# The first norm and split moved into edge counting, and counting in steps of six chunks, in a four-layer graph network on one core

## What is computed

```
h = relu(layernorm(x))
agg = segment_sum(h[src], dst);  cnt = segment_sum(1, dst)
y = agg / max(cnt, 1) @ W_l.T + b_l + h @ W_r.T
x = x + relu(batchnorm(y)) + h
```

## Time and profile before

| | us |
|---|---|
| median of 3 runs (1279.17 to 1279.27) | 1279.27 |
| the profiled execution, its own time | 1277.57 |
| its span, first to last instruction | 1275.8 |
| TensorE busy | 1146.9 (90%) |
| VectorE busy | 930.5 (73%) |
| ScalarE busy | 715.2 (56%) |
| GpSimd busy | 65.1 (5%) |
| first counting matmul starts | 28.08 |
| last tile of counts closed | 161.87 |
| first aggregation matmul starts | 193.63 |

### The profile page before, as it was taken

How to read it: one execution, slowest core, us unless ns; L and a number is a source line. 1 busy time by engine, 2 the same in 40 slices (tenths; PEclk the granted TensorE clock), 3 DMA queues, 4 the chain that set the end, 5 groups by cost and what they waited for, 6 DMA issues and landing times. The chain is left out here.

```text
span 1275.8 us, 17226 instructions
## 1 busy us (share of the span) xinstructions
PE 1146.9 (90%) x6001; PEld 721.6 (57%) x6001; DVE 930.5 (73%) x1686; ACT 715.2 (56%) x902; POOL 65.1 (5%) x115
## 2 busy tenths in 40 slices
PE   3999959997898995979999999969979999999996
PEld 2666634554775553434444544436536777777775
DVE  5999955002755787788989897875337888888885
ACT  1132267303556675337788786845126777777774
POOL 3000042100001200000000000000000000000000
PEclk8999968998999997989999999989989999999999
DMA  4000000003003000203111100000020011110002
GB/s 152 5 1 1 1 1 1 1 1 120 13 1 92 2 1 0 83 23 141 45 43 43 44 22 1 3 1 1 1 50 13 15 26 26 27 26 14 14 1 81
DMA packets 24770, 36.17 MB, mean 28 GB/s; under 512 B 11874, under 2 KB 13204, under 8 KB 24694
## 3 DMA queue, kind: packets, MB, share of 16 engines
q1 hardware_dynamic: 24694, 35.14, 9.1%
HBM read 26.03 MB, written 2.70 MB: 23 GB/s over the span
## 5 line engine op out<-in xcount | busy, mean ns | idle before, releaser
L59 PE MATMUL wide<-arena 125*125 (+9 forms) x2124 | 470.8, 371 | 34.0 <-DVE arena L904 13.3
L59 PEld LDWEIGHTS wide<-arena 125*125 (+5 forms) x2124 | 262.1, 131 | 219.3 <-issue 114.2
L1736 PE MATMUL wide<-arena 125*65 125x512 f32 (+1 forms) x480 | 182.3, 516 | 0.0
L1352 PE MATMUL wide<-ident,arena 125*125 125x125 f32 (+3 forms) x954 | 129.6, 282 | 14.0 <-ACT arena L603 4.7
L734 ACT ACTIVATE arena<-arena,b 125x1250 f32<-125x1250 f32 x80 | 106.7, 1336 | 60.1 <-PE wide L1736 56.0
L1251 DVE TENSOR_TENSOR arena<-wide,arena 125x1250 f32<-125x1250 f32 x80 | 116.7, 1459 | 30.1 <-PE wide L1726 30.0
L1352 PEld LDWEIGHTS wide<-ident,arena 125*125 125x125 f32 (+3 forms) x954 | 114.3, 185 | 24.5 <-issue 10.5
L813 ACT ACTIVATE arena<-wide 125x1000 f16<-125x1000 f32 x80 | 80.8, 1010 | 80.8 <-PE wide L1352 80.8
L1736 PEld LDWEIGHTS wide<-arena 125*65 125x65 f32 x480 | 63.4, 138 | 101.7 <-issue 95.3
L1313 DVE SCALAR_TENSOR_TENSOR arena<-wide,arena 125x1000 f16<-125x1000 f32 x80 | 95.9, 1198 | 33.9 <-ACT arena L813 33.9
L828 ACT ACTIVATE arena<-arena,neg_max,unit 125x1250 f32<-125x1250 f32 x80 | 114.3, 1429 | 10.7 <-DVE neg_max L1340 10.7
(11 more groups left out here) (250 smaller groups left out, 1236.5 us busy)
## 6 DMA issues: line engine op xcount, KB each, us to landing
arena<-rows_kept SPq DMA_DIRECT2D x16, 625.0 KB, 5.9
arena<-arena SPq DMA_DIRECT2D x40, 156.2 KB, 2.9
arena<-in_L_gnn_W SPq DMA_DIRECT2D x3, 1024.0 KB, 7.7
x_nm<-in_x SPq DMA_DIRECT2D x2, 1250.0 KB
out<-x_nm SPq DMA_DIRECT2D x1, 2187.5 KB
arena<-in_L_gnn_W_l SPq DMA_DIRECT2D x1, 1024.0 KB, 5.4
arena<-in_L_gnn_W_r SPq DMA_DIRECT2D x1, 1024.0 KB, 7.9
arena<-in_L_gnn_Wk SPq DMA_DIRECT2D x1, 1024.0 KB, 5.3
```

The source lines that it names most:

```text
L59: mm = pe.matmul(ps[0:rows, lo:hi], lhsT, rhs[:, lo:hi], start=start, stop=stop, skip_group_check=True)
L1352: return pe.transpose(dst, src, ident[0:k, 0:k])
L1736: m = pe.matmul(psW[1][0:VA, lo:hi], v_gat[0:ROWS, t, h, :], ring[n % RINGS][0:ROWS, lo:hi], start=(t == 0), stop=(t == TILES - 1))
```

## The change

- The bounds: each chunk's largest and smallest target, four chunks in each of 40 partitions, are compared with the tiles' edges there; TensorE turns the 0/1 result to one row per tile (10 partitions), where first and last chunk and the number of steps are found. Two small matmuls turn these to one partition and make the running sum.
- Counting: steps of six chunks, from each tile's own first chunk; columns behind the last chunk hold -1. The ring has six places. Counts of the preceding tile are turned after the first step (two parts) and after closing (the third). The last tile's mask is made by VectorE after counting.
- TensorE turns the weights after the bounds' small matmuls.
- Norm: statistics of two x tiles in each of tiles 1 to 5, their end in tiles 6 and 7; ScalarE takes the root in tile 5 and makes h and its upper part in tiles 6 to 8 (three, three, four tiles). h has ten places. VectorE makes seven lower parts right after its last chunk, three after the split of the degrees.
- The barrier between counting and aggregation is gone; the flag for counts over 2048 has a semaphore of its own, waited for at the end of the first block. GpSimd widens tiles 1 and 6 (also in the second layer), from when all turned counts are read, and adds h to x three tiles at a time behind that. h is transposed after each tile of the second aggregation block.

The diff, cut to its core:

```diff
-CHUNKS = 4
-GROUPS = E // (CHUNKS * CHUNK)
+CHUNKS = E // CHUNK
+PER = 4
+PARTS = CHUNKS // PER
+BODY = 6
+STEPS = (CHUNKS + BODY - 1) // BODY
+PADDED = CHUNKS + 2 * BODY
...
-        BY_ACT = (0, 1, 2, 3, 4, 6, 7, 8)
-        BY_POOL = (5, 9)
+        BY_ACT = (0, 2, 3, 4, 5, 7, 8, 9)
+        BY_POOL = (1, 6)
...
@@ block.gpsimd @@
+            pool.iota(order[0:TILES, 0, :].rearrange("p (g c) -> p g c", g=PER), pattern=[[1, PER], [PER, PARTS]], base=1, **many)
+            pool.iota(order[0:TILES, 1, :].rearrange("p (g c) -> p g c", g=PER), pattern=[[-1, PER], [-PER, PARTS]], base=CHUNKS, **many)
+            pool.iota(steps_at[0:TILES, :], pattern=[[BODY, STEPS - 1]], base=BODY, **many)
+            done(pool.memset(below[:, :], float(BODY)))
+            done(pool.affine_select(out=below[:, :], in_=below[:, :], compare_op=ALU.is_ge, fill=0.0, base=-1,
+                                    pattern=[[1, TILES + 1]], channel_multiplier=-1))
...
-            phase_end(pool, 1)
-            for t in range(TILES):
-                pool.wait_ge(S["h_made"], t + 1)
-                pool.tensor_tensor(x_nm[0:ROWS, t, :], x_nm[0:ROWS, t, :], h32[0][t % len(h32[0])][0:ROWS, :], ALU.add).then_inc(S["x_plus_h"], 1)
-            widen(0)
+            pool.wait_ge(S["counts_turn_read"], 3 * TILES)
+            for k in range(KD):
+                widen(0, k)
+                for t in range(3 * k, min(3 * k + 3, TILES)):
+                    pool.wait_ge(S["h_made"], t + 1)
+                    pool.tensor_tensor(x_nm[0:ROWS, t, :], x_nm[0:ROWS, t, :], h32[0][t][0:ROWS, :], ALU.add).then_inc(S["x_plus_h"], 1)
...
@@ block.scalar @@
+            for t in range(TILES):
+                act.wait_ge(S["tile_counted"], t + 1)
...
+                copy(cnt_f[t % 3][0:ROWS, :], psW[t % 2][0:ROWS, 0:N], accum_out=deg_col[0:ROWS, t:t + 1]).then_inc(S["counts_f32"], 1)
+                if t >= 1:
+                    turned_counts(t - 1, 2)
+                if t < TILES - 1:
+                    act.activation(mask[0:ROWS, t, :], psW[t % 2][0:ROWS, 0:N], ACT.Relu, bias=bar_c[0:ROWS, :], scale=-BARRED).then_inc(S["mask_made"], 1)
+                for r in range(2):
+                    turned_counts(t, r)
+                if t == 5:
+                    take_root(ROWS, 0, TILES)
+                if t == 6:
+                    act.wait_ge(S["ln_ready"], 1)
+                if 6 <= t <= 8:
+                    norm_first(*(range(0, 3), range(3, 6), range(6, TILES))[t - 6])
+            turned_counts(TILES - 1, 2)
...
@@ block.vector: bounds @@
+            tt(within[0][0:PARTS, :, :], chunk_most[0:PARTS, :].unsqueeze(2).to_broadcast(shape), edges[0], ALU.is_ge)
...
+            dve.wait_ge(S["edge_turns"], 1)
+            dve.wait_ge(S["consts_set"], 3)
+            done(tt(ordered[0:TILES, :, :], psS[1][0:TILES, 0:CHUNKS].unsqueeze(1).to_broadcast([TILES, 2, CHUNKS]), order[0:TILES, :, :], ALU.mult))
+            done(dve.tensor_reduce(ends2[0:TILES, :], ordered[0:TILES, :, :], AX, ALU.max))
+            first_c, n_steps, width, last_c = (span2[0:TILES, i:i + 1] for i in range(4))
+            ts(first_c, ends2[0:TILES, 1:2], -1.0, float(CHUNKS), ALU.mult, ALU.add)
+            done(ts(last_c, ends2[0:TILES, 0:1], 1.0, -1.0, ALU.max, ALU.add))
+            done(tt(first_c, first_c, last_c, ALU.min))
+            done(tt(width, last_c, first_c, ALU.subtract))
+            done(ts(passed[0:TILES, :], steps_at[0:TILES, :], width, None, ALU.is_le))
+            done(dve.tensor_reduce(n_steps, passed[0:TILES, :], AX, ALU.add))
+            ts(n_steps, n_steps, 1.0, 2.0, ALU.add, ALU.max).then_inc(S["edge_steps"], 1)
...
@@ block.vector: counting @@
+            for t in range(TILES):
+                if 1 <= t <= HEAD_HALF:
+                    x_stats(2 * t - 2)
+                    s = x_stats(2 * t - 1)
...
+                with dve.Fori(start, end, BODY) as n:
+                    for g in range(BODY):
+                        dve.wait_ge(S[f"hot{g}_free"], n + BODY)
+                        ts(hot_src[0:ROWS, g, :], iota_h[0:ROWS, :], e_col[0:ROWS, 1, c + g, :], None, ALU.is_equal)
+                        ts(hot_dst[0:ROWS, g, 0:ROWS], iota_h[0:ROWS, t * ROWS:(t + 1) * ROWS],
+                           e_col[0:ROWS, 0, c + g, :], None, ALU.is_equal).then_inc(S[f"hot{g}_made"], BODY)
...
@@ block.vector: after counting @@
+            for t in range(TILES - 3):
+                lower_part(0, t)
             dve.wait_ge(S["counts_f32"], TILES)
             split_cols(dve, done, parts[0:ROWS, :, :], split_rest[0:ROWS, :], deg_col[0:ROWS, :]).then_inc(S["deg_split"], 1)
+            for t in range(TILES - 3, TILES):
+                lower_part(0, t)
+            done(ts(mask[0:ROWS, TILES - 1, :], cnt_f[(TILES - 1) % 3][0:ROWS, :], 0.0, BARRED, ALU.is_equal, ALU.mult))
             dve.wait_ge(S["deg_wide"], 1)
...
-            phase_end(dve, 1)
-            big = has_big_count(dve)
-            ln_stats(0)
...
             for k in range(KD):
                 counts_of_block(0, k, big)
                 tt(aggT[:, k, :], psW[k % 2][:, 0:N], rdeg_b, ALU.mult).then_inc(S["agg_taken"], 1)
+                if k == 0:
+                    for t in range(TILES):
+                        turned_tile(0, t)
...
@@ block.tensor @@
+            pe.wait_ge(S["edge_steps"], 3)
+            pe.matmul(psS[1][0:1, 256:256 + TILES], span2[0:TILES, 0:1], ident[0:TILES, 0:TILES], start=True, stop=True)
+            pe.matmul(psS[1][0:1, 256 + TILES:257 + 2 * TILES], span2[0:TILES, 1:2], below[0:TILES, :], start=True, stop=True).then_inc(S["edge_turns"], 1)
             pe.wait_ge(S["w_in"], 32)
...
                 count_group(t, ends[t], True)
-                if t >= 2:
-                    turn_counts(t - 2, 2)
+                for r in range(2 if t >= 1 else 0):
+                    turn_counts(t - 1, r)
...
                 m.then_inc(S["tile_counted"], 1)
-                for r in range(2 if t >= 1 else 0):
-                    turn_counts(t - 1, r)
+                if t >= 1:
+                    turn_counts(t - 1, 2)
...
-            phase_end(pe, 1)
...
                         tile(k, j, cntT_16[l][(TILES * (l * KD + k) + j) % QUAD], j == 0).then_inc(S["cT_used"], 1)
+                        if l == 0 and k == 1:
+                            turn_h(0, j)
+                    if big is None:
+                        pe.wait_ge(S["big_set"], 1)
+                        big = has_big_count(pe)
...
-            big = has_big_count(pe)
-            turn_h(0, *range(TILES))
-            aggregate(0, big)
+            pe.wait_ge(S["mask_made"], TILES - 1)
+            big = aggregate(0)
```

More of the change, by code:

```diff
@@ L36 @@
 EXACT16 = 2048.0
-RING = 4
 TINY = 1e-30
@@ L518, in _ @@
                 pool.partition_all_reduce(kmaxa[:, half], kmax[:, half], 128, RMAX).then_inc(S["kmax_all"], 1)
-            phase_end(pool, 2)
-            widen(1)
+            phase_end(pool, 1)
+            for k in range(KD):
+                widen(1, k)
             pool.wait_ge(S["hT_made"], 3 * TILES)
@@ L860, in _ @@
-            done(dve.tensor_copy(group_row, psS[1][0:1, 0:2 * GROUPS]))
-            shape = [1, TILES, GROUPS]
-            largest = group_row[:, 0:GROUPS].unsqueeze(1).to_broadcast(shape)
-            smallest = group_row[:, GROUPS:2 * GROUPS].unsqueeze(1).to_broadcast(shape)
-            up, down = (r.unsqueeze(1).to_broadcast(shape) for r in (up_row, down_row))
-            lo, hi, tile_hi, n_groups, incl, excl, rest = (bnd[:, i, :] for i in range(7))
-            done(ts(tile_hi, tile_lo, float(ROWS), None, ALU.add))
@@ new lines, in _ @@
+            dve.tensor_copy(e_f[0:PARTS, :, :], e_raw[0:PARTS, :, :]).then_inc(S["edge_steps"], 1)
+            dve.wait_ge(S["edge_steps"], 1)
+            own = e_f[0:PARTS, 0, :].rearrange("p (g e) -> p g e", g=PER)
+            dve.tensor_reduce(chunk_most[0:PARTS, :], own, AX, ALU.max)
+            done(dve.tensor_reduce(chunk_least[0:PARTS, :], own, AX, ALU.min))
+            shape = [PARTS, PER, TILES]
+            edges = [edge[0:PARTS, i:i + TILES].unsqueeze(1).to_broadcast(shape) for i in range(2)]
@@ L1396, in count_group @@
             def count_group(t, n, first):
-                for g in range(CHUNKS):
-                    pe.wait_ge(S[f"hot{g}_made"], n + 1)
-                    wide_matmul(pe, psW[t % 2], ROWS, hot_dst[0:ROWS, n % 2, g, 0:ROWS], hot_src[0:ROWS, n % 2, g, :],
-                                first and g == 0, False).then_inc(S[f"hot{g}_free"], 1)
-            pe.wait_ge(S["edge_cols"], 1)
+                for g in range(BODY):
+                    pe.wait_ge(S[f"hot{g}_made"], n + BODY)
+                    wide_matmul(pe, psW[t % 2], ROWS, hot_dst[0:ROWS, g, 0:ROWS], hot_src[0:ROWS, g, :],
+                                first and g == 0, False).then_inc(S[f"hot{g}_free"], BODY)
             for t in range(TILES):
```

279 lines of the change are left out of this document (120 added, 159 removed).

## The result

The changed kernel took **1240.97 us** (median of 4 runs, 1240.37 to 1242.02) beside 1279.22 for the kernel before on the same chip: ratio 0.9702 [0.9685, 0.9719], a gain of 38.3 us where 30.0 were forecast. The profiled execution took 1241.29 us, its span is 1239.6; before they were 1277.57 and 1275.8. So the spans differ by 36.2 us.

A forecast was written before the change was run, and what follows sets the result against it. TensorE was taken to set counting, by little, with a serial chain before aggregation. Gains of 9.5 us up to the last closing and 20.5 after it, 30.0 off 1277.57, plus 1.7 for the median, gave 1249.3 us; range 1244 to 1257.

The forecast's parts named there:

- the step counts at 18.8: Start: three steps of VectorE's bounds chain wait for GpSimd's selects; step counts at 18.8, one-hots from 22.9 us.
- the 12.61 us of a counting tile: Counting: TensorE needs 18 x 0.575 + 2.26 = 12.61 us a tile; counting 124.5 against 133.8, gain 9.3.
- T to block 2: From T, the last counting tile's closing (forecast 152.3), to the second aggregation block's end: T + 35.4, gain 20.5 us.
- Rival (2): Start: only the bounds chain's two steps with both inputs in SBUF wait; first counting matmul 25.8, total 1247.3; chance 0.14.
- F: Time of the first counting matmul: 28.08 before, forecast 27.8, between 23 and 29; gain 0.3 us.
- 2.26 us is left: Counting tile: 2.26 us for closing, ten transposes of the preceding tile and the 0.70 loading the next loop's bound.
- 0.575 a chunk: Counting: TensorE's time for each of a tile's 18 chunks, from groups of 12 matmuls in 2.30 us.
- 12.5, just under 12.61: Counting, tiles 1 to 5: VectorE with two statistics needs 12.5 us, TensorE 12.61; cost taken as nothing.
- rival (1): Start: the bounds chain does not wait for GpSimd at all; first counting matmul at 23, total 1244.5; chance 0.06.
- (4): Rival: clock stays low through the first aggregation block, 21.7 instead of 13.2 us, 8.5 lost, total 1257.8; chance 0.05.
- The ring of six: Rival (3), counting: ring of six too short, nine us given back, total 1258.6; chance 0.07.
- the norm held up nobody: Rival (5), tiles 7 to 9: norm delays ScalarE's count reads, up to 2 us a tile, total 1255; chance 0.04.

The follow-up runs named there:

- selects_late: Changed kernel with GpSimd's three affine selects and their memset moved behind its other constants: 1240.79 us.
- before_turns: Kernel before with only the count transposes moved, two parts ahead of the bound's load and one behind the closing: 1268.96 us against 1277.04, ratio 0.9938.
- loads_ahead: Changed kernel with VectorE's two register loads of a tile placed ahead of that tile's statistics: 1236.76 us, ratio 0.9685 to the kernel before.
- weights_first: Changed kernel with the 32 weight transposes placed before TensorE's wait for the step counts: 1242.28 us.

## Why the prediction was right in sign and wrong in size

The gain was 38.3 us where 30.0 were forecast. The steps that failed are the step counts at 18.8 in the start, and the 12.61 us of a counting tile; the way from T to block 2 was right in sum. Two of the signs that the prediction named for being wrong showed: a first matmul before 25 (24.77) and a tile over 13 us (15.21).

- **Start, forecast 27.8, measured 24.77.** The failed step is "I let three steps wait so, and put the step counts at 18.8": they came at 16.48, though GpSimd was 0.9 later than before. One step waited, for 1.33 us. Rival (2) named the right direction and priced it at 25.8, but not the right step. The Trainium skill (SBUF — State Buffer, "Who interferes with whom") says that reductions never contend on this chip, and the trace of selects_late agrees (0.17 beside a select). It also lets a tensor_scalar in a two-port mode contend, which fits the 1.33 against 0.23; no run shows why the one-element form was not held. The small products and the handing over to the transposes took 0.7 us less than I allowed, the transposes 0.4 less, the tail behind them 0.4 more. What leads to T is not F but VectorE's first one-hot, forecast at 22.9 and measured at 20.12. Start and counting are therefore best read as one, 15.8 us gained where 9.5 were forecast.
- **Counting, forecast 124.5, measured 121.3.** Two terms failed. "2.26 us is left" for the rest of a tile kept the 0.70 of the bound's load, though the diff that I had before me puts transposes in front of it; before_turns shows the load covered. And 0.575 a chunk was 2.30 / 4, with a modelled end or a loop's turn in it; 18 chunks in tile 8 take 9.71 us and not 10.35. TensorE's tile is thus 11.17, and 12.61 - 0.70 - 0.64 = 11.27 accounts for it to 0.1. By this alone counting would be near 0.178 x 54 + 9 x 11.17 = 110 us, 14.4 under the forecast; the next two points took 11.2 back, so that the miss of 3.2 is the difference of two larger ones.
- **VectorE as the pace, costed at nothing.** "12.5, just under 12.61" was right for VectorE (12.30), so once TensorE's tile fell to 11.2, VectorE set tiles 1 to 4 and kept 0.6 us of the gain in the first and 1.1 in each of the others. With the loads out of the way, tiles 5 to 7 still took 3.2 over three of TensorE's tiles. Even without statistics VectorE's 18 x 0.617 = 11.1 is hardly less than TensorE's tile.
- **A stall that I had no term for.** VectorE's loads behind the norm's waits, 1.61 and 1.42 twice: 3.9 us in all by loads_ahead. The clock's fall in tile 5 is no part of it. The forecast had asked what stands behind each added wait on ScalarE, and not on VectorE.
- **T to block 2, forecast 35.4, measured 35.7.** Right in sum, by two errors. Aggregation began 1.5 late: 1.0 for the cast beside the lower parts, the rest because the split stood behind seven lower parts until 149.35 while the counts were out at 147.74. The Trainium skill's rule for two inputs in SBUF (same page and section) gave T + 5.9 where I took 5.5; the rows were on its side and went beyond it. Block 1 took 13.5 us (forecast 13.2), at a mean clock of 0.79. Block 2 took 15.2 and not 16.6, since a turned tile is 0.42 us (four transposes at 167.81, the next matmul at 168.23) and not 0.57.
- **The rivals.** The clock rose within the first block (4): 13.5 us and not 21.7. The ring of six held, the norm held up nobody (ScalarE's 7.83 and 9.17 busy in tiles 7 to 9, TensorE without idle in 8 and 9), all tiles took three steps, and hand-over was not paid by the chunk. Blocks 3 and 4 stayed at 10.9.
- **The range's low end**, 1244, was rival (1), an early start; it took the counting's 124.5 as known from below. The two errors came together, and the time lies 3.0 under it.

## What to carry to other kernels

Before costing a loop by its cadence, divide one straight-line group and one loop group by their counts: what differs belongs to the turn and changes with the number of turns, not with the work. A register load costs nothing while its engine has queued work; where nothing covers it, it cost 0.6 to 0.7 us here (0.70 for one on TensorE, 1.25 for two on VectorE; three at the start 3.09), so in every reordered program look at what stands ahead of each load. When two engines are near each other, a gain on one is worth only the distance to the other: work out both tiles before adding up. And look for the gaps of the engine that sets the pace: two falls of TensorE's clock (tile 5, and the first tile of weights_first) cost the total 0.3 us at most each, and VectorE's gaps cost it nearly in full.

## What of the hardware was not expected

- The 32 transposes of the weights ran at two paces under a granted clock that reads 1.00 throughout: ScalarE's reads stood 0.85 us apart until 22.14 in one profile of the changed kernel (6.36 us in all) and until 18.02 in the other (5.06), and about 0.5 apart afterwards. What sets the pace is left open.
- TensorE idled 4.2 us before those transposes with the clock at 1.00 afterwards; in tile 5 it idled 2.10 and the clock was at half from about 87 to 90 in one profile of the changed kernel, and stayed at 1.00 in the other. In weights_first an idle of 4.08 was followed by 0.50. The idle time alone doesn't tell which will come.
- A VectorE comparison of 26 columns was held 1.1 us by an affine select, a step on a single column not at all.
